# A mixture-of-experts kernel on one core: which arm of a two-way branch stands first in TensorE's program, and after which chunk the next body's tiles are transposed

## The reference

```python
x = x + jnp.tanh(g_xattn[0]) * _L0_xattn_ref(ctx_512, _layernorm(x, axis=-1), ...)
x = x + jnp.tanh(g_ffn[0]) * _L0_ffn_ref(_layernorm(x, axis=-1), ...)

# _L0_ffn_ref: 8 experts, hidden width 1024, 2 experts for each token
probs = jax.nn.softmax(jnp.einsum('ti,ei->te', xt, gate_w), axis=-1)
expert_weights, expert_indices = jax.lax.top_k(probs, 2)
expert_weights = expert_weights / expert_weights.sum(axis=-1, keepdims=True)
x1 = jax.nn.silu(jnp.einsum('ti,eoi->teo', xt, w1))
x3 = jnp.einsum('ti,eoi->teo', xt, w3)
expert_outs_all = jnp.einsum('teo,eio->tei', x1 * x3, w2)
out = sum over the 2 chosen experts of expert_weights * expert_outs_all
```

## Time and profile before

| | us |
|---|---|
| median of 3 runs | 771.75 |
| lowest and highest of them | 769.46, 771.84 |
| the profiled execution, its own time | 769.46 |
| its span | 767.7 |
| TensorE's matmuls busy within the span | 719.1 |

### The profile page before, as it was taken

How to read it: one execution, slowest core, us unless ns; L and a number is a source line. 1 busy time by engine, 2 the same in 40 slices (tenths; PEclk the granted TensorE clock), 3 DMA queues, 4 the chain that set the end, 5 groups by cost and what they waited for, 6 DMA issues and landing times.

```text
span 767.7 us, 13122 instructions
## 1 busy us (share of the span) xinstructions
PE 719.1 (94%) x4507; PEld 620.1 (81%) x4509; DVE 398.1 (52%) x1013; ACT 332.6 (43%) x649; POOL 200.5 (26%) x243
## 2 busy tenths in 40 slices
PE   7698798795999999999999999999999999999994
PEld 3494443574989998999989989999999899989993
DVE  2787779884554355425443564254535542644312
ACT  4797485512454244333533353335333533544221
POOL 4203824972204110403030304030403040203111
PEclk9758999998999999999999999999999999999997
DMA  8972253417516340543226324432363244303122
GB/s 311 411 302 111 110 220 115 138 15 282 178 80 199 121 112 33 135 160 69 109 58 236 69 109 121 166 74 104 62 232 69 109 138 152 67 1 69 42 27 28
DMA packets 24231, 98.76 MB, mean 129 GB/s; under 512 B 4560, under 2 KB 4816, under 8 KB 20368
## 3 DMA queue, kind: packets, MB, share of 16 engines
q1 hardware_dynamic: 14496, 70.54, 23.9%
q0 software_dynamic: 9568, 27.96, 16.1%
q10 hardware_dynamic: 144, 0.00, 0.0%
HBM read 77.50 MB, written 20.99 MB: 128 GB/s over the span
## 4 chain that ended last, share of the span: by engine, by line
issue 67%; POOL 11%; DVE 8%; PE 7%; POOLq 3%; DMA 2%; DVEq 1%; ACT 1%; SPq 0%
POOL x_body L528 4%; POOL out L534 4%; DVE front L1204 2%; POOL xb L474 2%; PE bank L627 1%; PE bank L674 1%; DMA out<-xb 1%; PE bank L600 1%; POOLq L542 1%; PE bank L683 1%; POOLq L331 1%; DVE scratch L1179 1%; PE bank L672 1%; PE bank L590 1%; DMA front<-ctxT 1%
## 5 line engine op out<-in xcount | busy, mean ns | idle before, releaser
L729 PE MATMUL bank<-xT_body_hi,w_hi 128*128 128x256 f32 (+1 forms) x960 | 275.8, 287 | 3.9 <-issue 3.6
L731 PE MATMUL bank<-xT_body_lo,w_hi 128*128 128x256 f32 (+1 forms) x960 | 275.3, 287 | 0.8 <-issue 0.8
L730 PE MATMUL bank<-xT_body_hi,w_lo 128*128 128x256 f32 (+1 forms) x960 | 275.1, 287 | 0.0
L729 PEld LDWEIGHTS bank<-xT_body_hi,w_hi 128*128 128x128 f32 x960 | 181.1, 189 | 10.7 <-issue 5.4
L730 PEld LDWEIGHTS bank<-xT_body_hi,w_lo 128*128 128x128 f32 x960 | 181.5, 189 | 3.6
L731 PEld LDWEIGHTS bank<-xT_body_lo,w_hi 128*128 128x128 f32 x960 | 181.2, 189 | 0.0
L1735 DVE TENSOR_TENSOR h<-bank,act_g 128x256 f32<-128x256 f32 (+1 forms) x120 | 52.4, 437 | 207.5 <-PE bank L731 202.2
L1116 ACT ACTIVATE hT_hi<-h 128x256 fp32r<-128x256 f32 (+1 forms) x120 | 51.4, 428 | 165.6 <-DVE h L1735 165.6
L1369 DVE TENSOR_TENSOR w_lo<-raw,w_hi 128x1024 fp32r<-128x1024 f32 x88 | 105.2, 1223 | 25.0 <-ACT w_hi L958 25.0
L1112 ACT ACTIVATE act_g<-bank 128x256 f32<-128x256 f32 (+1 forms) x120 | 46.5, 388 | 162.2 <-PE bank L731 162.0
L729 PE MATMUL bank<-w_hi,hT_hi 128*128 128x512 f32 (+1 forms) x280 | 114.1, 408 | 1.9 <-DVE hT_lo L1648 1.8
(11 more groups left out here) (307 smaller groups left out, 772.1 us busy)
## 6 DMA issues: line engine op xcount, KB each, us to landing
raw<-weights SPq DMA_DIRECT2D x24, 2048.0 KB, 10.4
raw<-xT SPq DMA_DIRECT2D x4, 1024.0 KB, 11.6
xb<-x SPq DMA_DIRECT2D x4, 1024.0 KB, 20.2
w_hi<-weights POOLq DMA_DIRECT2D x2, 2048.0 KB, 14.9
found<-xb SPq DMA_DIRECT2D x4, 1024.0 KB, 4.5
out<-xb SPq DMA_DIRECT2D x4, 1024.0 KB, 6.9
found<-scratch SPq DMA_DIRECT2D x1, 2092.0 KB, 30.2
front<-ctxT SPq DMA_DIRECT2D x4, 256.0 KB, 4.6
```

The costliest lines, as they stand in the source:

```text
L729: nc.tensor.matmul(out_ap, hi, hi_w, start=start, stop=False)
L730: nc.tensor.matmul(out_ap, lo, hi_w, start=False, stop=False)
L731: return nc.tensor.matmul(out_ap, hi, lo_w, start=False, stop=stop)
```

## The change

Two edits, both on TensorE. `turn_pair` moves from behind the up product of chunk 5 (the sixth) to that of chunk 6 (the seventh), in both arms. And the branch is turned round: the condition is `n != wide_at`, the pair arm stands directly behind it, and the wide arm in the `Else`.

```diff
@@ -888,7 +888,7 @@
                             if k > 0:
                                 pe.wait_ge(h_chunk, chunk[k - 1])
                             up_or_gate(k, 1, cols).then_inc(up_chunk_mm, 1)
-                            if k == 5:
+                            if k == 6:
                                 pe.wait_ge(x_body_set, next_nth)
                                 turn_pair(X_BODY)
                             if k == IC - 1:
@@ -898,10 +898,10 @@
                         y_chunk(IC - 2, tiles)
                         y_chunk(IC - 1, tiles)
 
-                    with pe.If(n == wide_at):
+                    with pe.If(n != wide_at):
+                        body(PAIR_COLS, PAIR_TILES)
+                    with pe.Else():
                         body(WIDE_COLS, WIDE_TILES)
-                    with pe.Else():
-                        body(PAIR_COLS, PAIR_TILES)
                     pe.nop()
```

## The result

| | before | after |
|---|---|---|
| median, us (11 runs each) | 771.5 | 773.22 |
| lowest and highest, us | 769.46, 773.07 | 772.49, 774.57 |
| ratio to before, 95% interval | | 1.0028 (1.0017 to 1.0038) |
| the profiled execution, its time and span | 769.46, 767.7 | 774.46, 772.7 |

The kernel became slower by 0.28%, about 2.2 us by the interval's middle (1.7 us between the medians). The two profiled executions are 5.0 us apart, more than the kernels are, because the one of before was its fastest and the one of after is among its slowest. Of the 5.0 us, 1.8 arise ahead of the first body, in code that is the same in both: the last early matmul starts at 185.24 and now at 186.99.

A forecast was written before the change was run, and what follows sets the result against it. TensorE, busy 94% of the span, bounds the kernel, so only breaks in its matmul row can be won. Terms -4.0 - 0.3 + 4.65 = +0.35 us on the 771.75 median give 772.1 us, range 767.2 to 774.8.

The forecast's parts named there:

- Part 1: Transposes behind chunk 6: TensorE's wait for ScalarE's normalised tiles goes in four bodies, 1.0 us each, -4.0 us.
- Part 2: Entry to the first body: code-wait breaks go, -1.5 us; half-level clock after waiting for VectorE, +1.2; sum -0.3 us.
- Part 3: End of first pair body: jump over the wide arm loads code once, 3.05 us idle plus 1.6 for the clock, +4.65.
- dividing the entry's 5.95 us: Entry branch: 3.6 us before the packet, shrinking to 0.9 at the jump with idle DMA engines, 0.95 for it, 1.4 after.
- No load at the jump: Rival: the loops' end is already loaded at the first pair body's end; sum -4.3 us, 767.4; chance 0.20.
- A load as dear as at the entry: Rival: first jump idles TensorE 5.75 us plus 1.7 for clock, entry gives nothing; +3.45, 775.2 us; chance 0.13.
- Every jump loading again: Rival: the jump ending each of 12 pair bodies loads code, some 3 us each; +32 us, 804; chance 0.02.
- the two-block rule: Instruction memory holds two 16 KB blocks; taken branches outside wait for a load, so all 12 pair bodies' jumps would stall.
- The clock staying up: Rival: no clock fall after the first jump's stop, or load near its lower bound; 770.5 or 769.5 us; chance 0.20.

The follow-up runs named there:

- e1: Only the transposes moved to the seventh chunk, order of the arms as before, against the kernel before: 766.97 us, ratio 0.9945.
- e2: Only the branch turned round, transposes left at the sixth chunk, against the kernel before: 777.52 us, ratio 1.0087.
- e10: Changed kernel plus an early run of TensorE through an empty arm of an outer loop, to load the loops' end: 773.36 us, ratio 1.0043 to before.
- e11: Changed kernel with both the earlier row placing of e6 and the early load of e10: 769.26 us, ratio 0.9982 to before.
- e12: e11 plus 12 matmuls into an unused bank while TensorE waits for the first body's tiles: 769.33 us, ratio 0.9979 to before.
- e4: e1 with the next expert's weight loads held back until the first body's tiles are ready: 766.96 us, ratio 0.9938 to before.
- e7: e4 plus the earlier row placing of e6 on VectorE: 771.75 us, ratio 0.9991 to before.
- e8: e7 plus 12 matmuls into an unused bank while TensorE waits for the first body's gathered tiles: 767.75 us, ratio 0.9968 to before.
- e5: Changed kernel with a thin wide arm, one matmul of three per product, so a shorter jump; total not to be compared: 727.67 us, one run.
- e3: Changed kernel with VectorE's row placing spread into idle gaps and the first body, using a few branches: 815.4 us, ratio 1.0578 to before.
- e6: Changed kernel with VectorE's rows placed and table entries read earlier, without any new branch: 768.41 us, ratio 0.9969 to before.
- e9: e1 plus 12 matmuls into an unused bank while TensorE waits for the first body's gathered tiles: 769.12 us, ratio 0.9985 to before.

## Why the prediction was right, and where it was off

The outcome, no change or a small loss, was forecast at 772.1 us, and 773.22 was measured, inside the range. Each stop was found where it had been put. The terms below are read from the two profiles and are larger together than the loss between the medians; where other runs give another value it is said.

**Part 1, -4.0 us.** Right. e1 alone gave -4.2 us, and nothing took the wait's place: in the changed kernel ScalarE ends its normalisation at 216.69 and the transposes start at 219.92, 3.2 us later, as worked out.

**Part 2, the entry, -0.3 us.** The mechanism was right, and one term was too small in this profile. The first body starts behind the last early matmul, the stop moves to the 37th matmul and is 4.29 us (4.6 expected), and that matmul starts 9.41 us behind the last early one, against 11.0: 1.6 us won, 1.5 predicted. What was mis-sized is the clock at the stop: I took 1.2 us, from half-level stretches of 3.4 us. It was at 0.50 for 6.6 us or more, and the 36 matmuls from the 37th to the end of the third chunk's up product took 6.72 us where they took 4.24: 2.5 us. By the two profiles the entry cost 0.9 us (from the last early matmul to the first second-layer one of the body 16.13 us, against 15.24). But the longer half level is not the change's own. In e1, with the old arms, it came at the entry too, and the same stretch took 15.8 us; in e2, with the new ones, it took 15.9. Between those two the entry gives and costs nothing.

**Part 3, +4.65 us.** Right in kind. The jump took 3.81 us where I worked out 3.25: 0.9 ahead of its packet and 1.4 behind it, as expected, and 1.5 for the packet (5.4% of 16 engines for 1.7 us) instead of 0.95. The stop was 3.45 us (3.05). The clock cost 2.7 us instead of 1.6: the first 72 matmuls of the second body took 11.24 us, and 8.53 before. In e2, with the half level for 3.4 us at that place, they took 10.06, which is 1.5 us and nearly the term as predicted; in e10, e11 and e12 they took 8.58. So the part was 1.7 us too small by this profile and about right by that of e2. e4, e7 and e8 show that dividing the entry's 5.95 us into a part that depends on the DMA engines and one that does not was sound. e5 shows that a short jump does not miss.

**A misread row.** The prediction says that the branch in front of the arms was evaluated 18 times. The run has 15 bodies, so the 18 records are 15 branches and three jumps at the wide arm's end. Nothing in the sum hangs on it.

**The rivals.** No load at the jump (0.20) is excluded by the 3.81 us. A load as dear as at the entry (0.13) is excluded too: 3.81 is far from 5.95, and the same jump took 3.4 to 4.0 in e2, e3, e6, e10, e11 and e12. Every jump loading again (0.02), which the two-block rule of the Trainium skill ("Runtime: NRT & Kernel Launch", section "Instruction fetch mechanics") would ask for, is excluded by 24 later records at up to 0.208 us. The clock staying up (0.20) did not happen in this profile. In those of e10, e11 and e12 it did, behind stops of 3.1 to 3.5 us at the same place, so that case deserved more than it got.

**The chances.** The change is 0.28% slower, at the edge of what counts as no change. The sum, +0.35 us, was 1.4 us too low by the medians and 1.8 by the interval's middle. Part 1 came out, so the miss is in what the branch costs: +6.7 us in e2 (5.5 to 8.0), where parts 2 and 3 together said +4.35. How much of it is the clock the profiles do not settle, since its term at one and the same place was 0 in three of them, 1.5 in e2 and 2.7 here.

**The better kernel** is the smaller change: with the transposes moved and the arms left as they were, 0.9945 of before. Holding the weights back on top of it (e4, 0.9938) is not clearly better.

## What to carry to other kernels

A far jump in this long unrolled program had a price once, at its first pass, and turning the arms round moved that place and did not remove it. Before taking out a stop, look for the engine that is late next: here 4.5 us of waiting for code hid VectorE, which was done with its first product only 1.7 us before TensorE's next use of it. And test two edits apart when they go in together: one was worth 0.55%, the other cost 0.87%. Before reading a clock term from two profiles, see where each stands among its kernel's executions: here 5.0 us lay between the profiles and 1.7 between the medians.

## What was not expected of the hardware

- The half level of TensorE's clock at a stop in the bodies lasted 3.4 us in some profiles (stops of 2.2 us in e6, 4.5 in e10) and 6.8 us in others (3.9 in e1, 4.3 in the changed kernel), and at three stops before the second body (e10, e11, e12, 3.1 to 3.5 us) it did not come at all. The length of the stop alone does not give it.
- A first far jump cost TensorE's sequencer 3.4 to 4.0 us in all thirteen cases of these runs with a DMA share of 0.02 to 0.70 over the jump, and 5.7 to 6.3 us in the three with 0.99 to 1.01 (before, e1, e9).
- A few more branches on VectorE (e3) raised the code packets of q14 from 14 to 84 and the time by 42 us beside the changed kernel. That VectorE's program had been near the length that is kept is likely, and not shown.
